# Moving loads and preparation work of a transformer block's prologue between queues and engines

## What is computed

```python
x = L0_attn_x
xn = _layernorm(x, axis=-1)
x = x + _L0_attn_ref(xn, ...) + _L0_ffn_ref(xn, ...)

def _features(x, omega, quad_nodes, quad_weights):        # attention: positive random features
    xn = x / jnp.maximum(jnp.linalg.norm(x, axis=-1, keepdims=True), 1e-12)
    proj = jnp.einsum('bhtd,rhdm->rbhtm', xn, omega)
    s = quad_nodes[:, None, None, None, None]
    sqrt_2s = jnp.sqrt(2.0 * jnp.maximum(s, 0.0))
    arg = jnp.clip(proj * sqrt_2s - s, -20.0, 20.0)
    feat = jnp.exp(arg) / np.sqrt(M).astype(np.float32)
    feat = feat * jnp.sqrt(jnp.maximum(quad_weights, 0.0))[:, None, None, None, None]

    xn = rms_norm(x, gamma_x)                             # soft mixture of experts
    se = rms_norm(slot_embeds, gamma_slot)
    logits = jnp.einsum('bsd,etd->bset', xn, se)
    dispatch = jax.nn.softmax(logits, axis=1)
    slots = jnp.einsum('bsd,bset->betd', xn, dispatch)
    h = jax.nn.gelu(slots @ w1, approximate=False)
    processed = h @ w2
    combine = jax.nn.softmax(logits.reshape(b, s, e * t), axis=-1)
    out = jnp.einsum('bnd,bsn->bsd', processed.reshape(b, e * t, d), combine)
```

## Time and profile before

| | |
|---|---|
| median of 3 runs | 474.83 us (474.27 to 476.93) |
| profiled execution, its own time | 474.87 us |
| its span | 473.1 us, so 1.77 us lie around the span |
| TensorE matmuls busy | 435.3 us (92%) |
| VectorE busy | 376.0 us (79%) |
| ScalarE busy | 314.4 us (66%) |
| GpSimd busy | 186.7 us (39%) |

### The profile page before, as it was taken

How to read it: one execution, slowest core, us unless ns; L and a number is a source line. 1 busy time by engine, 2 the same in 40 slices (tenths; PEclk the granted TensorE clock), 3 DMA queues, 4 the chain that set the end, 5 groups by cost and what they waited for, 6 DMA issues and landing times.

```text
span 473.1 us, 16005 instructions
## 1 busy us (share of the span) xinstructions
PE 435.3 (92%) x5712; PEld 359.2 (76%) x5712; DVE 376.0 (79%) x956; ACT 314.4 (66%) x577; POOL 186.7 (39%) x276
## 2 busy tenths in 40 slices
PE   3087999999999999999999999999999999999993
PEld 2056888888787888788887888878788887888782
DVE  5579788887988888887988889788898879677462
ACT  4226768676758667686766768675767767676761
POOL 4303444443533343353334345353334435334220
PEclk9589999999999999999999999999999999999998
DMA  2430202020020202011020202002020201102000
GB/s 54 99 65 1 46 13 48 24 46 21 12 51 11 53 13 44 24 32 24 11 55 11 44 22 44 17 6 55 11 50 17 44 11 24 34 2 58 1 13 12
DMA packets 45779, 14.46 MB, mean 31 GB/s; under 512 B 35640, under 2 KB 45624, under 8 KB 45752
## 3 DMA queue, kind: packets, MB, share of 16 engines
q1 hardware_dynamic: 45176, 13.77, 13.9%
q10 hardware_dynamic: 576, 0.33, 0.2%
HBM read 3.61 MB, written 2.10 MB: 12 GB/s over the span
## 4 chain that ended last, share of the span: by engine, by line
PE 68%; DVE 21%; issue 5%; SPq 2%; ACT 2%; DMA 1%; DVEq 1%
PE x L952 11%; PE p_s L1003 8%; PE x L1160 7%; PE x L1172 6%; PE p_t L1003 6%; DVE arg L747 6%; PE p_s L1015 5%; PE x L1151 4%; PE x L1015 3%; PE x L1094 3%; DVE slot_v L802 3%; PE p_s L988 2%; PE x L1129 2%; DVE s_sb L753 2%; PE x L1105 2%
## 5 line engine op out<-in xcount | busy, mean ns | idle before, releaser
L464 POOL TENSOR_TENSOR s_sb<-s_sb,causal 128x256 f32<-128x256 f32 x96 | 68.6, 734 | 112.3 <-ACT s_sb L538 110.3
L533 ACT ACTIVATE feat<-arg,f_bias 128x512 f32<-128x512 f32 x128 | 87.8, 717 | 0.2
L747 DVE TENSOR_SCALAR arg<-p_s,f_low,f_high 128x512 f32<-128x512 f32 x64 | 48.8, 803 | 13.4 <-PE p_s L988 13.4
L1003 PEld LDWEIGHTS p_s<-feat 64*64 64x64 f32 x1024 | 38.6, 132 | 18.2 <-issue 16.5
L311 POOL TENSOR_TENSOR qk_sq<-qkv 128x512 f32<-128x512 f32 x15 | 15.6, 1041 | 92.5 <-DVE qkv L724 92.5
L747 DVE TENSOR_SCALAR arg<-p_t,f_low,f_high 128x512 f32<-128x512 f32 x64 | 50.0, 801 | 0.0
L1003 PE MATMUL p_s<-feat 64*64 64x256 f32 (+3 forms) x1024 | 49.5, 309 | 0.0
L1003 PE MATMUL p_t<-feat 64*64 64x256 f32 (+3 forms) x1024 | 46.1, 296 | 0.0
L458 POOL TENSOR_TENSOR s_sb<-s_sb,causal 128x512 f32<-128x512 f32 x30 | 37.6, 1273 | 17.2 <-ACT s_sb L544 17.2
L1003 PEld LDWEIGHTS p_t<-feat 64*64 64x64 f32 x1024 | 41.5, 133 | 1.5
L1121 PEld LDWEIGHTS x<-xg,disp 128*128 128x128 f32 x256 | 29.8, 191 | 7.9 <-ACT disp L560 7.9
(11 more groups left out here) (155 smaller groups left out, 1021.7 us busy)
## 6 DMA issues: line engine op xcount, KB each, us to landing
out_dram<-out_sb SPq DMA_DIRECT2D x32, 64.0 KB, 2.1
xin<-in_L_attn_x_dram SPq DMA_DIRECT2D x31, 64.0 KB, 2.4
omega_f<-in_L_attn_omega_dram SPq DMA_DIRECT2D x16, 4.0 KB
se_rows<-n_L_ffn_slot_embeds_dram SPq DMA_DIRECT2D x1, 256.0 KB, 2.6
w_f<-in_L_ffn_w_dram SPq DMA_DIRECT2D x1, 256.0 KB, 3.6
w_sb<-in_L_ffn_w_dram SPq DMA_DIRECT2D x1, 256.0 KB, 3.6
stack_t<-stack SPq DMA_TRANSPOSE x16, 4.3
wqkv_f<-in_L_attn_Wqkv_dram SPq DMA_DIRECT2D x1, 192.0 KB, 4.1
```

The source lines that it names most:

```text
L464: pool.tensor_tensor(v, v, m, ALU.mult).then_inc(mb_ok, 1)
L533: nc.scalar.activation(feat[:, p % 4, :], arg[:, p % 4, :], ACT.Exp, bias=f_bias[:, 0:1]).then_inc(fe_ok, 1)
L747: nc.vector.tensor_scalar(arg[:, p % 4, :], bank, f_low[:, 0:1], f_high[:, 0:1], ALU.max, ALU.min).then_inc(cl_ok, 1)
L1003: mm = nc.tensor.matmul(dst[rows:rows + 64, u, o:o + hi - lo], f[:, T + keys:T + keys + 64], f[:, lo:hi], start=True, stop=True, skip_grou ...
```

## The change

- SyncE's queue: `se_rows`, `gs_bc` and now also `gx_bc` (before on ScalarE's queue) are issued directly behind Wqkv; omega is loaded once (8 DMAs), and after a wait for these the second copy is made by two DMAs from SBUF to SBUF; `gx_col` comes over from ScalarE's queue. `node_b` goes to ScalarE's queue.
- GpSimd: issues the four DMAs of `node_c` and `weight_c` as its first instructions; takes over the product of the embeddings with gamma (`se_g`), the fp16 copy and the subtraction of omega, and the product and split of w1; gives the zeroing of `vw` to VectorE. `residual` of row 0 stands before `place_v`.
- VectorE: the zeroing of `vw` stands first; `gs_rt` and the floor of the sums of squares stand before the nodes; `se_n` is one instruction on `se_g` in place of four; omega's two steps and w1's two are gone; `se_lo` stands before `stack_low`.
- ScalarE: the squares of the embeddings and their Ln and Exp stand before the roots of nodes and weights, `se_hi` before `stack_high`.
- TensorE: two zero matmuls in place of four behind the transposes of `se_n`.

```diff
+        se_g = sb("se_g", [128, NCH, 128])
...
-        def load_omega(eng, a):
+        def load_omega(eng):
 
             for u in range(2):
                 for h in range(2):
-                    row = 64 * u + 16 * a + HD * h
+                    row = 64 * u + HD * h
...
@@ SyncE
-            spread(node_b, nodes, R).then_inc(d_feat, 16)
-            for dst, src in ((node_c, nodes), (weight_c, weights)):
-                for h in range(2):
-                    sp.dma_start(dst[64 * h:64 * h + 64, :],
-                                  src.rearrange("(r m n) -> r m n", m=1, n=1).broadcast_to([R, M, 1])
-                                  ).then_inc(d_feat, 16)
+            sp.dma_start(se_rows[:, :, :], slot_embeds.rearrange("(c p) d -> p c d", p=128)).then_inc(d_se, 16)
+            spread(gs_bc, gamma_slot, C).then_inc(d_gs, 16)
+            spread(gx_bc, gamma_x, C).then_inc(d_gs, 16)
             sp.wait_ge(om_zero, 1)
-            load_omega(sp, 0)
-            load_omega(sp, 1)
-            sp.dma_start(se_rows[:, :, :], slot_embeds.rearrange("(c p) d -> p c d", p=128)).then_inc(d_se, 16)
-            spread(gs_bc, gamma_slot, C).then_inc(d_se, 16)
+            load_omega(sp)
             load_x((0, 1), T)
+            sp.wait_ge(d_om, 16 * 8)
+            for u in range(2):
+                o = 64 * u
+                sp.dma_start(omega_f[o + 16:o + 32, :, :], omega_f[o:o + 16, :, :]).then_inc(d_dup, 16)
+            spread(bout_bc, bout, C).then_inc(d_bo, 16)
             sp.dma_start(w1_f[:, :], w1).then_inc(d_w1, 16)
-            spread(bout_bc, bout, C).then_inc(d_bo, 16)
+            sp.dma_start(gx_col[:, :], gamma_x.rearrange("(a n) -> a n", n=1)).then_inc(d_w1, 16)
@@ GpSimd
+            for dst, src in ((node_c, nodes), (weight_c, weights)):
+                for h in range(2):
+                    pool.dma_start(dst[64 * h:64 * h + 64, :],
+                                   src.rearrange("(r m n) -> r m n", m=1, n=1).broadcast_to([R, M, 1])
+                                   ).then_inc(d_col, 16)
...
-            pool.memset(vw[:, :, :, :, :], 0.0).then_inc(vz_const, 1)
...
-            pool.wait_ge(d_om, 16 * 16)
+            pool.wait_ge(gs_s, 1)
+            pool.wait_ge(d_se, 16)
+            pool.tensor_tensor(se_g[:, :, :], se_rows[:, :, :],
+                               gs_rt[:, :].rearrange("p (a c) -> p a c", a=1).broadcast_to([128, NCH, C]),
+                               ALU.mult).then_inc(se_gs, 1)
+            pool.wait_ge(d_om, 16 * 8)
+            pool.wait_ge(d_dup, 32)
...
-            place_v((0, 0))
+            pool.wait_ge(om_s, 1)
+            pool.tensor_copy(omega_st[:, :, :], omega_f[:, :, :]).then_inc(om_s, 1)
+            pool.wait_ge(om_s, 2)
+            for u in range(2):
+                o = 64 * u
+                pool.tensor_tensor(omega_st[o + 32:o + 48, :, :], omega_f[o:o + 16, :, :],
+                                   omega_st[o:o + 16, :, :], ALU.subtract).then_inc(om_s, 1)
+            pool.wait_ge(om_s, 4)
             pool.wait_ge(d_bo, 16)
             residual((0, 0))
+            place_v((0, 0))
+            pool.wait_ge(d_w1, 32)
+            pool.tensor_scalar(w1_f[:, :], w1_f[:, :], gx_col[:, 0:1], None, ALU.mult).then_inc(w1_split, 1)
+            pool.wait_ge(w1_split, 1)
+            pool.tensor_copy(w1_hi[:, :], w1_f[:, :]).then_inc(w1_split, 1)
+            pool.wait_ge(w1_split, 2)
+            pool.tensor_tensor(w1_lo[:, :], w1_f[:, :], w1_hi[:, :].bitcast(F32), ALU.subtract).then_inc(w1_split, 1)
@@ VectorE
+            nc.vector.memset(vw[:, :, :, :, :], 0.0).then_inc(vz_const, 1)
             ln_stats(b0)
...
-            dve.wait_ge(om_s, 1)
-            nc.vector.tensor_copy(omega_st[:, :, :], omega_f[:, :, :]).then_inc(om_s, 1)
...
-            for c in range(NCH):
-                last = nc.vector.scalar_tensor_tensor(se_n[:, c, :], se_rows[:, c, :], small[:, CT_, 12 + c:13 + c],
-                                                      gs_rt[:, :], ALU.mult, ALU.mult)
-            last.then_inc(se_ok, 1)
+            dve.wait_ge(se_nw, 3)
+            dve.wait_ge(se_gs, 1)
+            nc.vector.tensor_tensor(se_n[:, :, :], se_g[:, :, :],
+                                    small[:, CT_, 12:16].rearrange("p (c a) -> p c a", a=1).broadcast_to([128, NCH, C]),
+                                    ALU.mult).then_inc(se_ok, 1)
...
-                if first:
-                    dve.wait_ge(d_w1, 32)
-                    nc.vector.tensor_scalar(w1_hi[:, :], w1_f[:, :], gx_col[:, 0:1], None, ALU.mult).then_inc(w1_split, 1)
-                    dve.wait_ge(w1_split, 1)
-                    nc.vector.scalar_tensor_tensor(w1_lo[:, :], w1_f[:, :], gx_col[:, 0:1], w1_hi[:, :].bitcast(F32),
-                                                   ALU.mult, ALU.subtract).then_inc(w1_split, 1)
@@ TensorE
-            for u in (0, 1, 0, 1):
+            for u in range(2):
                 nc.tensor.matmul(p_s[:, u, 0:384], ident[:, :], s_sb[:, 0, 0, :], start=True, stop=True)
```

More of the change, by code:

```diff
@@ L190, in build @@
         d_om = sem("d_om")
+        d_dup = sem("d_dup")
+        d_gs = sem("d_gs")
+        d_col = sem("d_col")
+        se_gs = sem("se_gs")
         d_se = sem("d_se")
@@ L592, in _ @@
             xt_high(b0)
+            act.wait_ge(d_se, 16)
+            for c in range(NCH):
+                last = nc.scalar.activation(junk[:, c, :], se_rows[:, c, :], ACT.Square,
+                                            accum_out=small[:, CS, c:c + 1])
+            last.then_inc(se_ss, 1)
+            act.wait_ge(se_cl, 1)
+            nc.scalar.activation(small[:, CT_, 4:8], small[:, CT_, 0:4], ACT.Ln).then_inc(se_a, 1)
+            act.wait_ge(se_a, 1)
+            nc.scalar.activation(small[:, CT_, 8:12], small[:, CT_, 4:8], ACT.Exp, scale=-0.5).then_inc(se_a, 1)
             act.wait_ge(f_in, 1)
@@ L837, in _ @@
             xt_low(b0)
-            dve.wait_ge(d_feat, 16 * 5)
+            dve.wait_ge(d_gs, 32)
+            nc.vector.scalar_tensor_tensor(gs_rt[:, :], gs_bc[:, :], float(C) ** 0.5, gx_bc[:, :], ALU.mult,
+                                           ALU.mult).then_inc(gs_s, 1)
+            dve.wait_ge(se_ss, 1)
+            nc.vector.tensor_scalar(small[:, CT_, 0:4], small[:, CS, 0:4], NORM_FLOOR, None, ALU.max).then_inc(se_cl, 1)
+            dve.wait_ge(d_feat, 16)
+            dve.wait_ge(d_col, 16 * 4)
             nc.vector.tensor_scalar(node_b2[:, :], node_b[:, :], 0.0, 2.0, ALU.max, ALU.mult)
@@ L885, in _ @@
                                     ALU.subtract).then_inc(se_l, 1)
+            stack_low(dve, b0)
+            dve.wait_ge(f_ln, 1)
+            nc.vector.tensor_tensor(f_bias[:, :], coef_ln[:, :], node_c[:, :], ALU.subtract).then_inc(f_ok, 1)
             ln_apply(b1)
```

53 lines of the change are left out of this document (14 added, 39 removed).

## The result

| | before | after |
|---|---|---|
| median of 4 runs each, same chip | 475.0 us | 469.25 us (468.7 to 471.47) |
| ratio | | 0.9879, 95% interval 0.9856 to 0.9903 |
| profiled execution, own time / span | 474.87 / 473.1 us | 468.73 / 467.0 us |

The change makes the kernel 1.2% faster.

A forecast was written before the change was run, and what follows sets the result against it. TensorE's matmuls, busy 92% of the span, were taken as the bound; the change could move only stretches where they are not. Milestone +4.0, w1 -2.0 and clock +1.0 made +3.0 on 474.87: 477.9 us, range 469.5 to 481.5.

The forecast's parts named there:

- GpSimd's four DMA issues: At the kernel's start: 1.0 us each, so all of GpSimd's constants come 4.0 us later.
- end of qkv's bias: In the prologue: VectorE ends the bias of qkv at 17.05 us, 5.1 later than before.
- VectorE alone, bias to milestone: VectorE's own work from qkv's bias to the first reduction over logits, without waits for GpSimd: 8.0 us.
- VectorE beside GpSimd: Same stretch: engines exclude each other for whole instructions, so VectorE waits 8.3 us, with gaps 8.8.
- milestone: Start of the first reduction over logits, ending the prologue: forecast at 33.9 us, 4.0 later than 29.89.
- w1: Row 0: with w1's split moved to GpSimd, `hidden` waits for `slot_lo` alone, saving 2.0 us.
- clock: TensorE stands 5 us before the logits and its clock may drop into row 0: +1.0 us, bounds 0 and 3.3.
- Rival 1: Prologue: VectorE and GpSimd hardly meet; 468.1 us with no waits paid, 472.5 with half; chance 0.27.
- Rival 2: Kernel's start: GpSimd's DMA issues cost only 0.4 us each, 2.4 less, 475.5 us; chance 0.20.
- Rival 3: The clock stays low into row 0, costing 3.3 us in place of 1.0, 480.2 us; chance 0.15.
- Rival 4: Kernel's start: VectorE's zeroing of `vw` holds up GpSimd's first DMA issue about 2 us, 479.9 us; chance 0.04.
- Rival 5: w1 or omega ends late on GpSimd and TensorE waits there; no size given; chance 0.01.

The follow-up runs named there:

- e5: Changed kernel plus a 640-column VectorE memset in front of the squares, so they start in the middle of GpSimd's scaling of omega; 473.13 us, one run.
- e9: Changed kernel plus six phases behind its last work, running small two-input VectorE products beside GpSimd idle, scalings, products, casts, memsets, differences; time not compared.
- e10: Changed kernel with GpSimd's residual right behind omega's scales and its other work held until behind row 1's layer norm; 467.83 us, ratio 0.9837.
- e4: Changed kernel with omega's two GpSimd scalings written as products with a broadcast tile; 475.0 us, one run.
- e6: Changed kernel with GpSimd's four DMA issues moved behind its constants; 468.06 us, ratio 0.9833.
- e13: The phases of e9 behind the changed kernel, with one-input maxima as VectorE's small instructions in place of two-input products; time not compared.
- e7: Changed kernel with residual first, omega's cast and subtractions held until row 0's `stack_low`, v copies and w1 until row 1's layer norm; 471.15 us, ratio 0.9919.
- e11: The kernel of e6 plus seven zero matmuls in TensorE's pauses of row 0; 466.38 us, ratio 0.9809.
- e15: Changed kernel with DMA issues behind GpSimd's constants, e10's waits and three zero matmuls in TensorE's pauses; 463.86 us, ratio 0.9744.
- e12: Changed kernel with DMA issues behind GpSimd's constants, e10's waits and seven zero matmuls in TensorE's pauses; 466.43 us, ratio 0.9809.

## Why the forecast was wrong, point by point

| step | forecast | measured |
|---|---|---|
| GpSimd's four DMA issues | 4.0 us | 2.9, constants 3.6 later |
| end of qkv's bias | 17.05 | 16.34 |
| VectorE alone, bias to milestone | 8.0 | 7.6 |
| VectorE beside GpSimd | +8.8 | +1.8 |
| milestone | 33.9 | 25.79 |
| w1 | -2.0 | -1.8 |
| clock | +1.0 | 0 in the profiled execution |

**The step that failed is "VectorE beside GpSimd".** It was put at +8.8 us and measured +1.8; of the 8.1 us by which the milestone came before 33.9, this step made 7.0, the earlier end of the bias 0.7 and VectorE alone 0.4. It rested on "the two engines exclude each other for whole instructions", read from the earlier trace rows, and gave each GpSimd instruction the same power to hold. Of the 8.3 us of waits summed there, 4.9 (squares, floor, `se_n`, `coef_pos`, Newton) were put beside omega's scalings and the cast behind them. Scalings hold little (e5; in e9 0.43 us at a time), and because they last 2.94 us and not 1.84, these steps were over before the cast began, but for the last 0.1 us. Here the waits measured 0.1. The other 3.4 (`qk_n`, the statistics of row 1, `stack_low`, `f_bias`) met cast, differences and residual and became 1.35, mostly because the statistics pass beside a difference (0.25 us for the two aggregates, as in e10), for which 2.3 had been set. The forecast was not consistent here: it let `se_lo` and the reductions pass since they read at most one operand from SBUF, and the statistics read one as well. To these 1.4 come 0.4 of the layer norm, for which nothing had been set.

's product and the earlier trace rows's memset case were real, and the floor beside `se_g` (0.91 us) came as forecast. What they could not carry is the other kinds: omega's scalings of 0.92 had an idle VectorE beside them, so no row told what a scaling holds. The mechanism of the forecast appears as soon as kind or phase changes: +3.3 us in e4, +2.5 in e5. This is also why the changed kernel's place is partly luck: half a microsecond on VectorE's side put it back to 473 in the one execution of e5.

Why a scaling holds so little stays open, and so does why in e9 it held a product begun 0.12 us after it (0.58 for 0.15), and in the kernel not `se_n`, begun 0.09 us after the second (0.68).

**The clock** was right as a danger and not met in the profile: its term hung on a pause of 5 us ahead of the logits, which came of the waits. TensorE went from the zero matmuls straight into the logits and was at 1.00 from 24.6. Of the four executions two took 469.76 and 471.47 at mean clocks of 0.987 and 0.986, the other two 468.7 at 0.996 and 0.998. If the spread is the clock's, the term is 0 to 2.8, within its bounds; where in those two the clock was low, no profile shows.

**Rivals.** Rival 1 came true, for a reason of kinds more than of pauses. That the profiled execution lies within 0.7 us of its 468.1 is luck in part: 1.8 us of waits were paid, and 0.7 at the bias and 0.4 of VectorE alone made up for them. Rival 2 (0.4 an issue) no: 0.67 to 0.77. Rival 3 no. Rival 4 no: the zeroing of `vw` took 1.76 us beside the issues, and in e6, where no memset of VectorE's runs beside them, the two pairs take the same 1.54 and 1.33 us. Rival 5 no: omega's steps and w1 end at 22.9 and 28.3, needed at 30.2 and 36.5.

**Range and chances.** By its own terms the upper end, rival 3 with the dearer copies, is 480.2 + 1.9 = 482.1 and not 481.5. A single row had decided between two outcomes 9 us apart. With the kinds unmeasured, the case of few waits deserved as much as the forecast.

## What to carry to other kernels

When work moves to GpSimd beside a chain of short VectorE instructions, price it by kind: a two-input operation or a cast costs the chain up to its own length at each second instruction (e9), a scaling by a column little (0.4 us at a time), a memset nothing for two-input forms and up to its length for one-input ones (e13). Put the holding kinds where VectorE makes reductions or statistics or is idle, and pin them there with a semaphore: half a microsecond of drift moved the milestone by 2.5 us, and a pin at the wrong place (e7) lost what it was to save. Here a shorter prologue paid out only while TensorE's clock stayed up (e6 against e11 and e15); zero matmuls of 2.1 us in pauses of 2.9 did it (e15), 4.9 us of them made TensorE the bound (e12).

## What the runs showed of the hardware

- GpSimd's scaling by a column is slow but porous: 512 float32 columns take 1.56 us, a product of two tiles 1.26; the scaling stretches to 1.79 when VectorE works beside it, the product does not.
- Beside products, differences or casts of GpSimd (1.26, 1.26 and 0.61 us, 512 columns) each second one of a train of small VectorE instructions waits until a GpSimd instruction ends; the eight take 4.87, 4.87 and 2.24 us for 0.67 (e9).
- VectorE's statistics and reductions are not stretched beside them (aggregates 0.25 us beside a difference; the reduction of e4 0.69 beside a product).
- Why a scaling holds one VectorE instruction (0.58 for 0.15 us in e9) and then lets the others pass stays open.
